# Expert feed-forward in a routed-expert kernel: tiles of 512 and 384 tokens in place of 256, and GpSimd's gather and add in another order

## The reference

```
x = x + 0.5 * ffn(layernorm(x))
x = x + linear_attention(layernorm(x))      # 16 heads of 16, causal cumulative sum of k v^T
x = x + 0.5 * ffn(layernorm(x))
```

## Time and profile before

| | us |
|---|---|
| median of 3 runs (lowest, highest) | 3151.95 (3150.39, 3155.76) |
| profiled execution, its own time | 3149.82 |
| its span, first to last instruction | 3148.1 |
| mean granted TensorE clock | 0.963 |

### The profile page before, as it was taken

How to read it: one execution, slowest core, us unless ns; L and a number is a source line. 1 busy time by engine, 2 the same in 40 slices (tenths; PEclk the granted TensorE clock), 3 DMA queues, 4 the chain that set the end, 5 groups by cost and what they waited for, 6 DMA issues and landing times. The chain is left out here.

```text
span 3148.1 us, 68785 instructions
## 1 busy us (share of the span) xinstructions
PE 2983.8 (95%) x26142; PEld 2873.9 (91%) x26143; DVE 1454.1 (46%) x3401; ACT 1290.6 (41%) x2586; POOL 1073.6 (34%) x1501
## 2 busy tenths in 40 slices
PE   6769999999999999979999995999999999999998
PEld 6669999999999999977888884999999999999998
DVE  7833434343434434325777775434434343434343
ACT  4633434343434434324555453434434343434343
POOL 3833333434333333330121112343433333333333
PEclk6579999999999999989999997999999999999999
DMA  7432222222323231120111103323223123312211
GB/s 252 141 97 38 64 37 60 41 67 33 68 30 70 35 66 29 32 64 28 42 55 43 55 29 95 67 33 69 40 61 69 31 34 67 69 32 67 34 27 31
DMA packets 144275, 181.29 MB, mean 58 GB/s; under 512 B 13808, under 2 KB 118000, under 8 KB 144176
## 3 DMA queue, kind: packets, MB, share of 16 engines
q0 software_dynamic: 53184, 73.51, 14.6%
q1 hardware_dynamic: 81856, 97.30, 10.0%
q10 hardware_dynamic: 9136, 9.18, 0.9%
HBM read 108.63 MB, written 71.31 MB: 57 GB/s over the span
## 5 line engine op out<-in xcount | busy, mean ns | idle before, releaser
L1051 DVE TENSOR_TENSOR e_hid<-e_ps,e_gate 128x512 f32<-128x512 f32 x540 | 373.2, 691 | 1034.8 <-ACT e_gate L1011 1027.7
L85 PE MATMUL e_ps<-e_xT_hi,e_wb_hi 128*128 128x256 f32 x2176 | 611.5, 281 | 0.0
L87 PE MATMUL e_ps<-e_xT_hi,e_wb_lo 128*128 128x256 f32 x2176 | 611.2, 281 | 0.0
L86 PE MATMUL e_ps<-e_xT_lo,e_wb_hi 128*128 128x256 f32 x2176 | 611.2, 281 | 0.0
L85 PE MATMUL e_ps<-e_xT_hi,c_wa_hi 128*128 128x256 f32 x2144 | 601.6, 281 | 4.4 <-DVE e_xT_lo L1045 3.0
L86 PE MATMUL e_ps<-e_xT_lo,c_wa_hi 128*128 128x256 f32 x2144 | 600.6, 280 | 0.0
L87 PE MATMUL e_ps<-e_xT_hi,c_wa_lo 128*128 128x256 f32 x2144 | 600.3, 280 | 0.0
L1055 DVE TENSOR_TENSOR e_h_lo<-e_hid,e_h_hi 128x512 fp32r<-128x512 f32 x540 | 374.5, 693 | 377.8 <-ACT e_h_hi L1013 298.0
L1011 ACT ACTIVATE e_gate<-e_ps 128x512 f32<-128x512 f32 x540 | 322.7, 598 | 530.7 <-PE e_ps L87 497.5
L1013 ACT ACTIVATE e_h_hi<-e_hid 128x512 fp32r<-128x512 f32 x540 | 342.1, 633 | 421.5 <-DVE e_hid L1051 412.6
L891 POOL DMA_INDIRECT x<-e_yrow,e_y_token x140 | 226.0, 1614 | 551.8 <-ACT e_yrow L1024 528.8
(11 more groups left out here) (261 smaller groups left out, 5565.5 us busy)
## 6 DMA issues: line engine op xcount, KB each, us to landing
raw<-w SPq DMA_DIRECT2D x204, 256.0 KB
normed_rows<-r_xn SPq DMA_DIRECT2D x8, 1056.0 KB, 5.4
normed_rows<-mi_xn SPq DMA_DIRECT2D x8, 1056.0 KB, 4.7
r_xin<-x SPq DMA_DIRECT2D x8, 1024.0 KB, 7.9
x<-r_xin ACTq DMA_DIRECT2D x8, 1024.0 KB, 5.2
mi_x<-x SPq DMA_DIRECT2D x8, 1024.0 KB, 8.2
out<-mi_x SPq DMA_DIRECT2D x8, 1024.0 KB, 5.3
e_xrow<-normed_rows,e_token POOLq DMA_INDIRECT x274
```

Source lines behind the costliest of these rows:

```text
L85: pe.matmul(out, a[0], b[0], start=first, stop=False)
L86: pe.matmul(out, a[0], b[1], start=False, stop=False)
L87: return pe.matmul(out, a[1], b[0], start=False, stop=last)
L1051: dve.tensor_tensor(hid[:, j % 2, :], ps3[j % 2][:], gate[:, j % 2, :], ALU.mult).then_inc(hid_ready, 1)
```

## The change

Tiles have 4 or 3 units of 128 tokens. An expert's number of units is its count divided by 128 and rounded up, at least 13, and 15 becomes 16. It is written as a first tile of 3 units, then `big` tiles of 4, then `small` tiles of 3, with both at least 1; Router.tiles computes both numbers by integer steps. In phase 1 a matmul moves 512 or 384 columns, and each hidden block has a bank of its own (8 steps f in place of 4 steps j). In a first tile a weight piece is split in each of the 8 steps, between silu and the high part on ScalarE, and the last 4 pieces behind the transposed rows. Every tile gathers, transposes and adds 4 units, also one of 3 (its fourth unit is added with zero or old data to spare rows). The next rows' token numbers and weights pass through one more pair of buffers (next_token, next_weight). So GpSimd's tile(g) now issues the gathers of tile g, and then the adds of tile g - 2 in place of g - 1; x_turned is raised twice for a turn. yrow(g) therefore waits for a y_meta that is raised in GpSimd's tile(g + 2), behind the gathers of that tile.

```diff
-TS = 256
-TPE = CAP // TS
-MIN_TILES = 2
+BIG, SMALL = 4, 3
+UPE = CAP // P
+MIN_UNITS, GAP = 13, 15
...
-    def tiles(self, dve, ntile, first_tile):
+    def tiles(self, dve, table):
...
+        dve.tensor_scalar(units, unitsi, float(MIN_UNITS), None, ALU.max)
+        dve.drain()
+        dve.tensor_scalar(odd, units, float(GAP), None, ALU.is_equal)
+        dve.drain()
+        dve.tensor_tensor(units, units, odd, ALU.add)
+        dve.drain()
+        dve.tensor_scalar(oddi, units, 3.0, -2.0, ALU.mult, ALU.add)
+        dve.drain()
+        dve.tensor_scalar(oddi, oddi, 3, None, ALU.bitwise_and)
...
+        dve.scalar_tensor_tensor(units, odd, -3.0, units, ALU.mult, ALU.add)
+        dve.tensor_scalar(table.small[:], odd, 1.0, None, ALU.add)
+        dve.drain()
+        dve.tensor_scalar(units, units, -6.0, 0.25, ALU.add, ALU.mult)
+        dve.drain()
+        dve.tensor_copy(table.big[:], units)
...
+                    tile(e, s, SMALL, True, e * UPE, f)
+                    with eng.Fori(0, big) as t:
+                        tile(e, s, BIG, False, e * UPE + SMALL + t * BIG, eng.snap(f + 1 + t))
+                    behind = eng.snap(f + 1 + big)
+                    at = eng.snap(e * UPE + SMALL + big * BIG)
+                    with eng.Fori(0, small) as t:
+                        tile(e, s, SMALL, False, at + t * SMALL, eng.snap(behind + t))
...
+                def meta(g):
+
+                    pool.wait_ge(y_added, WORDS * g + 16)
                     wait_alone(pool, held, g + 1, k.passed)
                     pool.tensor_copy(y_weight[:], held_weight[:])
                     pool.tensor_copy(y_token[:], held_token[:]).then_inc(y_meta, 1)
...
+                    wait_alone(pool, y_meta, g + 1, k.passed)
+                    pool.tensor_copy(held_weight[:], next_weight[:])
+                    pool.tensor_copy(held_token[:], next_token[:]).then_inc(held, 1)
+
+                def hold(e, subs, at, g):
+
+                    wait_alone(pool, held, g + 2, k.passed)
+                    wait_alone(pool, x_loaded, WORDS * g + WORDS, k.passed)
+                    pool.tensor_copy(next_weight[:], xrow[:, :, bass.ds(e + D, 1)].rearrange("p s o -> p (s o)"))
...
+                def tile(e, s, subs, first, at, g):
+                    wait_alone(pool, x_turned, KD * g + KD, k.passed)
+                    pool.tensor_copy(token[:], slot_token[:, bass.ds(at, BIG)]).then_inc(token_ready, 1)
                     wait_alone(pool, token_ready, g + 1, k.passed)
                     gather(g)
-                    add_last(g)
-                    wait_alone(pool, y_meta, g + 1, k.passed)
-                    hold(e, at, g)
+                    meta(g)
+                    hold(e, subs, at, g)
                     wait_alone(pool, y_kept, g + 1, k.passed)
-                    add()
+                    add(BIG)
...
-                pool.nop().then_inc(y_kept, 1)
+                pool.nop().then_inc(y_kept, 2)
                 wait_alone(pool, held, 1, k.passed)
-                add()
+                add(1)
...
+                    for f in range(KF):
+                        pe.wait_ge(hid_ready, KF * g + f + 1)
+                        for ps, base in ((ps1[f % 2], 0), (ps3[f % 2], F)):
+                            for kk in range(KD):
+                                ins = mm3(pe, ps[:, 0:n], wt(kk * 2 * F + base + f * P),
+                                          (xT[0][:, kk, 0:n], xT[1][:, kk, 0:n]), kk == 0, kk == KD - 1)
                         ins.then_inc(h_made, 1)
-                    turn(32 * g + 64)
-                    pe.wait_ge(y_kept, g + 1)
+                    turn(WORDS * g + 2 * WORDS)
+                    pe.wait_ge(y_kept, g + 2)
+                    for f in range(KF):
+                        pe.wait_ge(h_ready, KF * g + f + 1)
+                        for sub in range(subs):
+                            own = slice(sub * P, (sub + 1) * P)
+                            ins = mm3(pe, psy[:, sub, :], (h[0][:, f, own], h[1][:, f, own]), w2t(f),
+                                      f == 0 and sub % 2 == 0, f == KF - 1 and (sub % 2 == 1 or sub == subs - 1))
                     ins.then_inc(y_made, 1)
...
+                def tile(e, s, subs, first, at, g):
+                    n = subs * P
+                    if first:
                         act.wait_ge(y_made, g + 1)
+                    for f in range(KF):
+                        act.wait_ge(h_made, KF * g + f + 1)
+                        act.wait_ge(hid_ready, KF * g + f + 1)
+                        act.activation(gate[:, f % 2, 0:n], ps1[f % 2][:, 0:n], ACT.Silu).then_inc(gated, 1)
+                        if first:
+                            high_w(e, s, f)
+                        act.wait_ge(hid_ready, KF * g + f + 3)
+                        act.activation(h[0][:, f, 0:n], hid[:, f % 2, 0:n], ACT.Copy).then_inc(h_high, 1)
+                    high_x(KD * g + 2 * KD + 1)
+                    if first:
+                        for q in range(KF, PIECES):
                             high_w(e, s, q)
                     act.wait_ge(y_made, g + 2)
-                    act.wait_ge(y_meta, g + 2)
+                    act.wait_ge(y_meta, g + 3)
```

More of the change, by code:

```diff
@@ L436, in tiles, with __init__ @@
         dve.drain()
-        dve.tensor_copy(cnti, cnt)
+        dve.tensor_copy(unitsi, units)
         dve.drain()
-        dve.tensor_scalar(cnti, cnti, TS.bit_length() - 1, None, ALU.logical_shift_right)
+        dve.tensor_scalar(unitsi, unitsi, P.bit_length() - 1, None, ALU.logical_shift_right)
         dve.drain()
-        dve.tensor_scalar(cnt, cnti, float(MIN_TILES), None, ALU.max)
+        dve.tensor_scalar(units, unitsi, float(MIN_UNITS), None, ALU.max)
         dve.drain()
-        dve.tensor_copy(ntile[:], cnt)
-        dve.tensor_tensor_scan(scan, cnt, zero, 0.0, ALU.add, ALU.add)
-        dve.memset(first_tile[:, 0:1], 0.0)
+        dve.tensor_scalar(odd, units, float(GAP), None, ALU.is_equal)
         dve.drain()
-        dve.tensor_copy(first_tile[:, 1:E + 1], scan)
+        dve.tensor_tensor(units, units, odd, ALU.add)
[4 more added lines that the diff above has]
+        dve.drain()
+        dve.tensor_copy(odd, oddi)
+        dve.drain()
[5 more added lines that the diff above has]
+        dve.tensor_copy(table.big[:], units)
+        dve.scalar_tensor_tensor(count, odd, 2.0, units, ALU.add, ALU.add)
+        dve.drain()
+        dve.tensor_tensor_scan(scan, count, zero, 0.0, ALU.add, ALU.add)
+        dve.memset(table.first[:, 0:1], 0.0)
+        dve.drain()
+        dve.tensor_copy(table.first[:, 1:E + 1], scan)
+class TileTable:
+    def __init__(self, m, i):
+        self.big = m.sb(f"big{i}", [P, E], I32)
+        self.small = m.sb(f"small{i}", [P, E], I32)
+        self.first = m.sb(f"first{i}", [P, E + 1], I32)
 class Setup:
@@ L846, in expert_phase, with experts @@
         w_low = m.sem("w_low")
[L848 removed]
+        WORDS = 16 * BIG
+        def experts(eng, tile):
             with eng.Fori(0, E // 2) as i:
@@ L880, in gather @@
                 def gather(g):
-                    wait_alone(pool, held, g + 1, k.passed)
-                    for sub in range(2):
+                    wait_alone(pool, next_held, g + 1, k.passed)
+                    for sub in range(BIG):
                         pool.indirect_dma_start(
@@ L886, in gather, with add @@
                             bounds_check=ROWS - 1, oob_is_err=True).then_inc(x_loaded, 16)
-                def add():
-                    for sub in range(2):
+                def add(subs):
+                    for sub in range(subs):
                         pool.indirect_dma_start(
@@ L940, in _ @@
+                pool.tensor_copy(y_weight[:], held_weight[:])
+                pool.tensor_copy(y_token[:], held_token[:]).then_inc(y_meta, 1)
+                wait_alone(pool, y_meta, n + 2, k.passed)
+                wait_alone(pool, y_kept, n + 2, k.passed)
+                add(SMALL)
+                wait_alone(pool, y_added, WORDS * n + WORDS + 16 * SMALL + 16, k.passed)
+                wait_alone(pool, x_loaded, WORDS * n + WORDS, k.passed)
             @block.tensor
             def _(pe):
-                pe.nop().then_inc(x_turned, 1)
+                pe.nop().then_inc(x_turned, KD)
@@ L947, in turn @@
                     for half in range(KD):
-                        for sub in range(2):
-                            at = half * TS + sub * P
-                            ins = pe.transpose(psx[:, at:at + P], xrow[:, sub, half * P:(half + 1) * P], k.ident[:])
-                    ins.then_inc(x_turned, 1)
-                def tile(e, s, t, g):
+                        for sub in range(BIG):
+                            ins = pe.transpose(psx[:, half, sub * P:(sub + 1) * P],
+                                               xrow[:, sub, half * P:(half + 1) * P], k.ident[:])
+                        ins.then_inc(x_turned, 1)
+                def tile(e, s, subs, first, at, g):
```

(15 more changed lines are left out.)

191 lines of the change are left out of this document (78 added, 113 removed).

## The result

The changed kernel takes 3136.46 us (median; 3135.04 to 3139.46) against 3151.95 before. The ratio is 0.995, with a 95% interval of 0.9935 to 0.9965. It is faster, by 15 us (half a per cent) and not by the predicted 150, and it lies 76 us above the upper end of the range. The profiled execution spans 3137.5 us against 3148.1, so 10.6 us is what the two traces have to explain.

A forecast was written before the change was run, and what follows sets the result against it. It took TensorE, with matmuls in flight for 95% of the span, to bound the kernel. From 3149.8 us, -141 - 17 - 14 + 8 + 5 + 5 + 2 + 2 = -150 gave 3000 us, range 2975 to 3060.

The forecast's parts named there:

- The spacing does not depend on 160 or 256 moving columns, so it is that of the stationary operand: TensorE, float32r: 116 ns at 160 columns, 116.7 at 256, so wider matmuls cost their columns alone; phase 1 -141 us.
- The slope and the 2.5 ns on top: Matmul cost at full clock: 2.4 GHz column rate plus 2.5 ns, giving 215.8 ns at 512 columns and 162.5 at 384.
- The half-clock row: TensorE at 1.2 GHz: 256 columns take 213 ns, one column per cycle, so the moving side is not slower than that.
- Loops: one more inner loop an expert, 16 entries ... I take +2: Expert phases: entering one more inner loop per expert costs +2 us, between 0 and 5 us.
- The rival of wide matmuls: Phase 1: spacing grows with columns, 233 and 175 ns, so phase 1 gains only -55, total 3086 us; chance 0.08.
- Units and phase 2: Phase 2: 264 units against 270, six fewer of 24 matmuls of 256 columns each: -17 us.
- Turn: Transposes between phases 1 and 2: 80 turns of 1.09 us against 135 of 0.65, so 0 us.
- Row waits: TensorE's waits for gathered rows inside a phase disappear because gathers are issued most of a tile earlier: -14 us.
- First tiles: Weight pieces in first tiles: VectorE takes 2.22 us a step against TensorE's 1.95, 0.5 us late each: +8 us.
- Elementwise chain: Ordinary tiles, silu to high part: about 1.66 us at 384 columns against TensorE's 1.95; cost 0, upper bound 18 us.
- GpSimd: Gathers and adds in a tile of 3: about 19 us against 25.1, y_meta 8.0 us behind the turn; cost 0.
- Starts, ends, Router.tiles: Phase edges and routing: phase starts +5 us in all, phase ends +5 us, Router.tiles' extra instructions +2 us.

The follow-up runs named there:

- experiment 1: The changed kernel with its outer loop over pairs of experts written out, so no branch back between pairs is left: 3093.63 us, 0.9815 of before.
- Experiment 3: The kernel before plus a phase of independent matmul series of varied width, type and place; its time is not the kernel's; float32r spacing 228.9 ns at 512 columns.
- experiment 6: The kernel before plus a phase of 24-matmul series at 12 offsets of the moving operand; time not the kernel's; spacing moved 3% at 512 columns, 6% at 256.
- Experiment 2: The kernel before, tiles still 256 tokens, with GpSimd's new order alone (gathers of the tile, then adds of the tile two back): 3138.19 us, 0.9956 of before.
- experiments 2 and 7: The second of these, 7: the kernel before with its outer loop over pairs of experts written out and nothing else: 3149.94 us, 0.9991 of before.

## Why the prediction was wrong

Expert phases by the trace, from the start of each group of matmuls to that of the next, in us; "written out" is experiment 1. The row of phase 1 holds the waits for rows in front of the turns.

```
                       before    after   written out   predicted   measured (written out)
phase 1 and row waits  1550.7   1490.0      1476.9        -147        -74
phase 2                 775.2    796.9       765.8         -17         -9
turns                    59.3     70.2        70.2           0        +11
starts, middle, end                                        +12        +15
outer branch                                                +2        +46 (span 3137.5 - 3091.4)
sum                                                       -150        -11
```

**"The spacing does not depend on 160 or 256 moving columns, so it is that of the stationary operand": the step that failed.** Experiment 3 measured 111.7 ns at 160 columns and 117.7 at 256. The trace of the kernel before had shown it too. The prediction's 116 ns is an average over 15 steps of which the first is odd: two of the 16 matmuls take 0.45 us together, one 0.27,

```profile
1542.88 0.45 PE L407 MATMUL mi_xv<-mi_r_picked_col,mi_r_picked_row 128*128 128x160 f32 x2
```

so the first step is 0.18 us, and the other 14 are (2.02 - 0.45) / 14 = 112 ns. 256 columns, at 116.7, were therefore above the floor and already paid by the column (0.434 ns each above 256 in experiment 3), so a wider matmul had little to give: it gets 227 to 233 ns at 512, not 215.8, and 173.4 to 176.6 at 384, not 162.5. Over 2304 and 5376 matmuls this is 1471 us against the 1371 of the sum. The kernel before was 1523 by the same count (117.5 on average, where 1512 was assumed). So the term was -52, not -141. The rest of the -74 is 22 us less in the gaps before the turns, 14 of them the waits for rows.

**The slope and the 2.5 ns on top** were taken from float32 matmuls of 264 and 128 columns, which are another form. bf16 in experiment 3 does give 215.8. The half-clock row, one column per cycle, was right for 1.2 GHz and says nothing of 2.4: the sum read a limit at full clock from a row at half clock.

**"Loops: one more inner loop an expert, 16 entries ... I take +2": the second step that failed.** The inner loops cost nothing that shows (the gaps between tiles are 13 us in all written out, 18 before), and the loop that mattered was another: the outer one, which the change doesn't touch but whose body it makes longer, from 592 to 1104 matmuls. 46 us in the profiled executions, 43 in the medians. No rival named it.

**The rival of wide matmuls, 233 and 175 ns, had the right spacing and a wrong sum.** It had 0.08. Measured were 227 to 233 and 173 to 177. But 2304 x 233 ns is 537 us and not the 516 of the prediction, so this rival should have said -34 for phase 1 and 3107 us in all, not -55 and 3086. That its -55 is near the measured -52 is luck: the wide matmuls were a little faster than it had them (1471 us, not 1478) and the kernel before slower (1523, not 1512). Its evidence against was the false step above.

**Units and phase 2: -17 predicted, -9 measured.** The 264 units and 6336 matmuls for 6480 came as predicted. The time per matmul, gaps included, went from 119.6 to 120.9 ns on average, +8 us over what was counted. The places of the tensors had moved, and in experiment 6 256 columns vary from 113.3 to 120.1 with the place. That places are the cause here was not tested.

**Turn: 0 predicted, +11 measured.** Eight transposes take 0.79 us to the first e_psy (608.06 to 608.85), four took 0.41. The 0.65 us of the prediction held the turn and the slower phase 2 of the tile, so it was too large for what 80 turns replace.

**Row waits: -14, right.** The waits of the trace went from 21 to 2, and the 14 us inside the phases are gone. Experiment 2 gave 14 us of the median as well, but as a balance of more terms than this one.

**First tiles: +8 predicted, about +2.** First tiles take 0.1 us more than ordinary ones in phase 1 over e_wb (17.06 against 16.96) and, written out, 0.2 more over c_wa. TensorE's list of waits has none for e_hid, so VectorE keeps up.

**Elementwise chain: 0, right.** It is 1.65 us at 384 columns against TensorE's 2.08, where "shrinks by a quarter of the streaming part" gave 1.66.

**GpSimd: 0, right.** Gathers are 1.32 to 1.40 us apart, y_meta is up 6.6 us behind the first copy, and nothing waits for it.

**Starts, ends, Router.tiles: +12 predicted, +15 measured**, from the first turn (191.8 to 195.3), between the phases (559.2 to 567.4) and behind the last e_psy (12.3 to 16.0). These edges vary by as much from trace to trace: in the traces of experiments 2 and 7, with tiles of 256, the first turn is at 188.7 and 194.5.

## What to carry to other kernels

Whether a matmul is bound by its floor or by its columns has to be read from a difference larger than the reading's error: compare single starts, of the same type and clock, and not the average over a group, in which one odd first step made 112 ns look like 116; here 6 ns of 117 decided about 90 us. A change that makes a loop's body longer changes the price of the branch back: count the matmuls of every enclosing body before and after, compare the packets of the instruction queue, and look for waits of issue behind the branch. Where they stand, write the loop out or keep its body short; the written-out loop moves as many packets, but without a stall. And when two edits come together, price and run them apart: here GpSimd's order alone gave 14 us, as much as the two together, because the outer branch hid what the width gave. And when a kernel gets a new buffer, measure the matmuls it leaves alone: in experiment 2 their spacing moved too.

## What was not expected of the hardware

- float32r matmuls at full clock: 111.7 ns from start to start up to 192 columns, 117.7 at 256, 173.3 at 384, 228.9 at 512. bf16 at 512: 215.8. The Trainium skill (TensorE: Matmul & The Clock Gate, Wait, "56ns, not 53.3ns?") has N / 2.4 GHz plus about 2.5 ns, by which an estimate for 512 is 215.8: this trace agrees for bf16, and for float32r the measurement is 6% above it.
- The place of the moving operand shifts this by up to 3% at 512 columns and 6% at 256, by no rule found here.
- A branch back over a body of 848 matmuls or more costs 3.7 to 5.6 us, and in the changed kernel 3.2 to 5.5 us of matmuls at 1.2 GHz behind it; over 752 or fewer, 1.2 us or less.
